# A recurrent condition and a routed FFN on one core: inputs on two queues, projections two blocks ahead, tanh straight into the next round's start, shared weights in halves

## What is computed

```python
def step(prev_h, xp_t):                  # recurrence; the state is 256 wide
    next_h = jnp.tanh(xp_t + prev_h @ Wh)
    return (next_h, next_h)
xp = einsum('ntd,dh->nth', x, Wx) + b    # x is (2, 1024, 256)
h = scan(step, h0, xp)                   # over the 1024 positions
# FFN on h: one shared expert and 8 routed ones, the best 2 of them for a token
shared = silu(h @ shared_w1.T) @ shared_w2.T
gates = softmax(top2(h @ gate_w.T))
selected = sum over the 2 experts e: gate_e * (silu(h @ w1_e) @ w2_e)
out = x + shared + selected
```

## Time and profile before

| | |
|---|---|
| timed runs | 383.47, 385.0, 388.58 us (median 385.0) |
| the profiled execution | 381.38 us, of it 379.7 us span |
| PE busy | 356.2 us, 94% |
| ACT busy | 244.1 us, 64% |
| DVE busy | 200.2 us, 53% |
| POOL busy | 108.5 us, 29% |

### The profile page before, as it was taken

The page is one execution under the profiler, slowest core; times in us unless marked ns, Lnnn a source line. Parts: engine busy times, 40 slices in busy tenths (PEclk is TensorE's granted clock), DMA queues, the critical chain, the costliest instruction groups (busy, mean ns, idle before and its releaser), DMA issues.

```text
span 379.7 us, 8904 instructions
## 1 busy us (share of the span) xinstructions
PE 356.2 (94%) x2458; PEld 253.0 (67%) x2459; DVE 200.2 (53%) x415; ACT 244.1 (64%) x478; POOL 108.5 (29%) x99
## 2 busy tenths in 40 slices
PE   5989999997997998999999999999999999999981
PEld 4758889964664675666667666667766666666660
DVE  0089999979996988964333323333323333232310
ACT  3777788888556778865555665556665556665530
POOL 1100010000276788600123333223333133332241
PEclk9999999999999999999999999999999999999996
DMA  6999999607697979999898998889988989989992
GB/s 194 422 421 434 428 407 334 194 4 124 87 199 182 225 180 226 235 194 196 176 129 153 168 155 155 147 149 156 158 149 154 148 142 158 148 159 147 152 127 28
DMA packets 158173, 73.50 MB, mean 194 GB/s; under 512 B 140736, under 2 KB 155200, under 8 KB 156992
## 3 DMA queue, kind: packets, MB, share of 16 engines
q1 hardware_dynamic: 146672, 59.83, 66.9%
q0 software_dynamic: 6864, 9.11, 16.9%
q10 hardware_dynamic: 4608, 4.20, 4.1%
HBM read 23.68 MB, written 16.53 MB: 106 GB/s over the span
## 4 chain that ended last, share of the span: by engine, by line
PE 80%; ACT 6%; DMA 5%; issue 3%; DVE 2%; another core or an unknown queue 1%; ACTq 1%; POOL 0%; SPq 0%; DVEq 0%; POOLq 0%
PE py L1138 32%; PE z L1033 30%; PE z L1047 8%; PE z L982 3%; PE z L1014 3%; DMA space<-recurrence_w 2%; DMA space<-space 2%; ACT space L799 1%; ACT space L876 1%; PE px L1025 1%; PE py L982 1%; PE z L995 1%; DMA space<-x_cols 1%; ACTq L896 1%
## 5 line engine op out<-in xcount | busy, mean ns | idle before, releaser
L1138 PE MATMUL py<-w_slots,space 128*128 (+1 forms) x1272 | 148.4, 273 | 7.4 <-DMA space<-recurrence_w 3.7
L1033 PE MATMUL z<-w_slots,x 128*128 (+1 forms) x636 | 145.9, 379 | 0.8 <-issue 0.8
L1138 PEld LDWEIGHTS py<-w_slots,space 128*128 128x128 f16 x1272 | 123.8, 98 | 33.1 <-issue 3.5
L1033 PEld LDWEIGHTS z<-w_slots,x 128*128 128x128 f16 x636 | 62.1, 98 | 65.0 <-issue 1.2
L453 POOL DMA_INDIRECT out<-space x37 | 57.5, 1553 | 157.0 <-issue 65.2
L876 ACT ACTIVATE space<-z,tile_scales 128x512 f32<-128x512 f32 x106 | 71.8, 678 | 41.3 <-PE z L1033 34.1
L582 DVE SCALAR_TENSOR_TENSOR recurrence_w<-space,tile_scales,recurrence_w 128x512 f16<-128x512 f32 x54 | 40.5, 750 | 71.7 <-ACT recurrence_w L881 65.6
L582 DVE SCALAR_TENSOR_TENSOR space<-space,tile_scales 128x512 f16<-128x512 f32 x52 | 39.0, 750 | 57.7 <-ACT space L881 42.4
L528 DVE SCALAR_TENSOR_TENSOR w_slots<-w_slots,w_scale 128x1024 f16<-128x1024 f32 x36 | 46.2, 1283 | 1.3 <-issue 0.3
L881 ACT ACTIVATE recurrence_w<-space,tile_scales 128x512 f16<-128x512 f32 x54 | 39.0, 722 | 8.7 <-ACT space L876 2.5
L430 POOL DMA_INDIRECT sorted_rows<-space x32 | 39.1, 1221 | 17.5 <-issue 13.1
(11 more groups left out here) (114 smaller groups left out, 178.9 us busy)
## 6 DMA issues: line engine op xcount, KB each, us to landing
w_slots<-weights SPq DMA_DIRECT2D x9, 2048.0 KB, 30.5
sorted_rows<-pad_row SPq DMA_DIRECT2D x1, 5070.0 KB, 60.2
space<-x_rows ACTq DMA_DIRECT2D x16, 128.0 KB
out<-space ACTq DMA_DIRECT2D x16, 128.0 KB
space<-x_cols SPq DMA_DIRECT2D x1, 1024.0 KB, 8.6
space<-recurrence_w SPq DMA_TRANSPOSE x54
space<-space SPq DMA_TRANSPOSE x52
x<-sorted_rows SPq DMA_TRANSPOSE x39
```

Source lines behind the costliest of these rows:

```text
L1033: last = nc.tensor.matmul(Z[u % 2][h][:], x16[:, u, x_part, k], weight(f, k * HID + h * BANK, BANK, part), start=k == 0 and x_part == 0 an ...
L1138: last = nc.tensor.matmul(PY[p][:, 0:D], hiddenT[:, p, low, q], weight(f, MATRIX + q * D, D, part), start=q == 0 and not low and part == 0 ...
```

## The change

- **Inputs.** ACT's queue now starts Wx, h0 and the bias; SP starts the first block of x at once. The last four blocks of x come in two transfers, and FFN 0's weights in two halves, each half between two transfers of x. The gate's weights come behind x and FFN 0.
- **Warm-up.** PE does six matmuls on a tile of ones before its first projection. POOL sets that tile first.
- **Round 0.** Four projections ahead of the first guess step; then PE does the guess step first and the projection of two blocks ahead behind it, and ACT does the two tanh first and `project_out` behind them.
- **Starts.** The last tanh of rounds 0 and 1 writes 126 columns straight to the next round's starting column. `next_start` on ACT and `start_ok` are gone, and PE waits for the tanh of each half.
- **Finding.** DVE finds FFN 0 in two halves and 6 of the 8 chunks of FFN 1. FFN 0 is reduced, scaled and its first split done alone, before FFN 1 is looked at. There are 7 batches in place of 6. ACT's finds begin 2 chunks earlier in the weights, so 10 chunks are left after round 2 in place of 8: one find of two chunks before tile 0, and one in each of tiles 1 to 4 (before: two, then tiles 1 and 2). ACT's loop in round 1 is written out. The scratch of the finds moves to the end of `space`.
- **Late scales and splits.** The last `find_scales` moves from g = 4 to g = 5 and stands with `route_scales`. Split 24 moves from g = 6 to g = 5 and is all DVE's; the ones behind it move up by one.

```diff
-ARRIVALS = ((0, 1), (1, 2), (2, 4), (4, BLOCKS))
+ARRIVALS = ((0, 1), (1, 2), (2, 4), (4, 6), (6, BLOCKS))
...
-EARLY_WIDES = 6 * WIDES - 2
-BOUND_BATCHES = ((0, 2), (2, 3), (3, 4), (4, 5), (5, 6), (6, FFNS))
-FOUND_BY_DVE = BOUND_BATCHES[0][1]
-WIDE_FINDS_FROM = FOUND_BY_DVE + L // CHUNKS
-SPLIT_FROM = 6
-LATE_WIDES = BOUND_BATCHES[-1][0] * WIDES
-LATE_SPLITS = tuple(range(LATE_WIDES + (3 * n + 1) // 2, LATE_WIDES + (3 * n + 4) // 2) for n in range(TILES - 2 - SPLIT_FROM))
+EARLY_WIDES = 22
+
+
+BOUND_BATCHES = ((0, 1), (1, 2), (2, 3), (3, 4), (4, 5), (5, 6), (6, FFNS))
+FOUND_BY_DVE = 2 * CHUNKS - 2
+WIDE_FINDS_FROM = FOUND_BY_DVE + L
+LATE_FINDS_FROM = WIDE_FINDS_FROM + 2 * L
+LATE_FINDS = (FFNS * CHUNKS - LATE_FINDS_FROM) // 2
+SPLITS_AT = {3: (22, 23), 5: (24,), 6: (25, 26), 7: (27,), 8: (28, 29), 9: (30,), 10: (31,), 11: (32, 33), 12: (34,), 13: (35,)}
+HIGHS_FROM = 6
...
-    return (min(f, WIDE_FINDS_FROM) - FOUND_BY_DVE) * CHUNKS + max(f - WIDE_FINDS_FROM, 0) * WIDES
+    return min(f * CHUNKS, WIDE_FINDS_FROM) - FOUND_BY_DVE + max(f * CHUNKS - WIDE_FINDS_FROM, 0) // 2
...
-        magnitudes = ys[:, 2:4].rearrange("p u d -> p (u d)").bitcast(BF16)
...
+        assert at[0] <= SPACE - CHUNK - 1
+        magnitudes = space[:, SPACE - CHUNK - 1:SPACE - 1].bitcast(BF16)
...
-            sp.dma_start(wx_sb, wx).then_inc(wx_in, 16)
...
+            load_x(0)
+            sp.dma_start(wh_sb, wh).then_inc(wh_in, 16)
+            load_x(1)
+            load_x(2)
+            load_weights(0, 0, CHUNKS // 2, w_up_in)
+            load_x(3)
+            load_weights(0, CHUNKS // 2, CHUNKS, w_in[0])
+            load_x(4)
             sp.dma_start(gate_sb[:], gate_cols).then_inc(gate_in, 16)
-            for f in range(FFNS):
-                sp.dma_start(w_slots[:, f * CHUNKS + 2:(f + 1) * CHUNKS + 2].rearrange("p s c -> p (s c)"),
-                             weights[f]).then_inc(w_in[f], 16)
+            for f in range(1, FFNS):
+                load_weights(f, 0, CHUNKS, w_in[f])
...
+            nc.gpsimd.memset(ones[:], 1.0).then_inc(consts, 1)
...
-                if n == 0:
-                    pool.wait_ge(bound_ok, 2)
-                else:
+                if n < 2:
+                    pool.wait_ge(bound_ok, n + 2)
+                if n > 0:
                     pool.wait_ge(found, found_upto(end))
...
-            for f in range(FOUND_BY_DVE):
-                last = find_largest(f)
-            last.then_inc(bound_ok, 1)
+            find_largest(0, 0, CHUNKS // 2, w_up_in)
+            find_largest(0, CHUNKS // 2, CHUNKS, w_in[0]).then_inc(bound_ok, 1)
             find_scales(0)
             link(nc.vector.tensor_copy(tile_scales[:, 0:TILES].rearrange("p t s -> p s t"),
                                        ffn_scales[:, :, 0:1].broadcast_to([P, 3, TILES])))
-            split_upto(FOUND_BY_DVE * WIDES)
+            split_upto(1)
+            find_largest(1, 0, FOUND_BY_DVE - CHUNKS, w_in[1]).then_inc(bound_ok, 1)
+            split_upto(WIDES)
...
-                elif g < TILES - 2:
-                    if g == 3:
-                        split_upto(LATE_WIDES)
-                    elif g == 4:
-                        find_scales(5)
-                        route_tiles()
-                    elif g == 5:
-                        route_scales()
+                elif g == 4:
+                    route_tiles()
+                elif g == LATE_FINDS:
+                    find_scales(len(BOUND_BATCHES) - 1)
+                    route_scales()
                 if g >= AHEAD:
                     shared_y(g - AHEAD)
-                if SPLIT_FROM <= g < TILES - 2:
-                    for c in LATE_SPLITS[g - SPLIT_FROM]:
-                        split(c, high_by_act=c in highs_by_act)
+                for c in SPLITS_AT.get(g, ()):
+                    split(c, high_by_act=c in highs_by_act)
...
+            nc.scalar.dma_start(wx_sb, wx).then_inc(wx_in, 16)
+            nc.scalar.dma_start(states[:, :, 0, 0:B], h0_cols).then_inc(h0_in, 16)
+            nc.scalar.dma_start(bias_sb[:], bias).then_inc(bias_in, 16)
...
-            for m in range(K):
-                project_out(0, m)
+            for n in range(K + 1):
+                project_out(n // K, n % K)
             for i in range(BLOCKS):
                 for u in range(2):
-                    if i + 1 < BLOCKS:
-                        project_out(i + 1, u)
                     for m in range(K):
                         act.wait_ge(z_mm[m], i * 2 + (u + 1))
-                        nc.scalar.activation(guess[:, 1 - u, m], ahead[i % 3][m][:, u * COLS:(u + 1) * COLS], ACT.Tanh,
-                                             bias=bias_sb[:, m:m + 1]).then_inc(h_ok[m], 1)
+                        if i * 2 + u + 1 == L:
+                            nc.scalar.activation(next_start(m), ahead[i % 3][m][:, u * COLS:(u + 1) * COLS - B], ACT.Tanh,
+                                                 bias=bias_sb[:, m:m + 1]).then_inc(h_ok[m], 1)
+                        else:
+                            nc.scalar.activation(guess[:, 1 - u, m], ahead[i % 3][m][:, u * COLS:(u + 1) * COLS], ACT.Tanh,
+                                                 bias=bias_sb[:, m:m + 1]).then_inc(h_ok[m], 1)
+                    n = i * K + u + K + 1
+                    if n < BLOCKS * K:
+                        project_out(n // K, n % K)
...
+                if c % CHUNKS == 0 or c == FOUND_BY_DVE:
+                    act.wait_ge(w_in[c // CHUNKS], 16)
...
-            def next_start(r, ends):
-
-                for k in range(K):
-                    act.wait_ge(h_ok[k], r * L)
-                act.sem_inc(act_waited, 1)
-                nc.scalar.copy(states[:, :, 0, B:COLS], ends[:, :, 0:COLS - B]).then_inc(start_ok, 1)
...
+                        if starts_next and u == 1:
+                            nc.scalar.activation(next_start(m), Z[p][m][:, u * COLS:(u + 1) * COLS - B], ACT.Tanh).then_inc(h[m], 1)
+                        else:
+                            nc.scalar.activation(column(m, i * 2 + u + 1), Z[p][m][:, u * COLS:(u + 1) * COLS], ACT.Tanh).then_inc(h[m], 1)
...
-                with act.Fori(0, steps // 2) as j:
-                    for p in range(2):
-                        step_pair(z_mm, h_ok, r, j * 2 + p, p, find_at, chunks)
-                for i in range(steps, L // 2 - 1):
-                    if i % steps == 0:
-                        act.wait_ge(w_in[first_found + i // steps], 16)
+                for i in range(L // 2 - 1):
...
-            act.wait_ge(w_in[LAST], 16)
-            for c in range(WIDES // 2):
-                act.wait_ge(found, found_upto(LAST) + c)
-                find_last(c)
+            find_last(0)
...
-                if g <= WIDES // 2:
-                    c = WIDES // 2 + g - 1
-                    act.wait_ge(found, found_upto(LAST) + c)
-                    find_last(c)
-                if SPLIT_FROM <= g < TILES - 2:
-                    c = highs_by_act[g - SPLIT_FROM]
+                if g < LATE_FINDS:
+                    find_last(g)
+                if g >= HIGHS_FROM and g in SPLITS_AT:
+                    if g == HIGHS_FROM:
+                        act.wait_ge(tiles_ok, 1)
+                    c = SPLITS_AT[g][0]
...
+            pe.wait_ge(consts, 1)
+            for _ in range(WARM_UP):
+                nc.tensor.matmul(PX1[:, 0:P], ones[:], ones[:], start=True, stop=True)
...
-            for m in range(K):
-                project(0, m)
+            for n in range(2 * K):
+                project(n // K, n % K)
             pe.wait_ge(guess_ok, 3)
             for i in range(BLOCKS):
                 for u in range(2):
-                    if i + 1 < BLOCKS:
-                        project(i + 1, u)
                     guess_step(i, u)
+                    if i + 2 < BLOCKS:
+                        project(i + 2, u)
...
+                        if k == 0 and (chained or u):
...
-                pe.wait_ge(start_ok, r)
...
-            pe.wait_ge(start_ok, SPECULATIVE_ROUNDS - 1)
```

46 lines of the change are left out of this document (21 added, 25 removed).

## The result

The changed kernel takes 389.5 us (median of 20 runs, 385.8 to 392.6), the kernel before in the same comparison 384.2 (20 runs). The ratio is 1.0136, 95% interval 1.0111 to 1.0160: 5.2 us slower, under 2% but clear of 1. The forecast was 383.9. The profiled execution took 388.2, its span 386.5 us (before 379.7).

The account below looks back on a forecast made before the run. PE and DVE together bound the time to the shared FFN, then the hand-over to the routed tiles: 3.0 us gained at the start, 1.9 returned, so 1.1 off, 383.9 against 385.0; range for 8 in 10, 378 to 388.

Parts of the forecast that it names:

- the hand-over: From POOL's last scatters to SP's loads of sorted rows and the routed tiles: returns 1.9 us of the gain.
- First projection at 3.8: Inputs: x's first block is issued one transfer earlier, so PE's first projection begins near 3.8 instead of 4.25.
- first guess step at 8.0: Warm-up: four projections cost 4.2 us, so the first guess step comes at 8.0 instead of 8.75, gain 0.75.
- slow bound: Warm-up without effect: the four projections ahead of the first guess step cost 6.0 us.
- 1.14 a step: Round 0: all 15 step intervals become short, 17.1 us in place of 18.46, gain 1.4.
- Starts and loop: Dropped copy lets round 1 begin 0.4 us earlier; ACT's written-out loop saves 0.11 at 8 positions, 0.9 us.
- end of the early splits at 76.6: DVE's early work takes 61 us from 15.5, ending at 76.6 instead of 79.68, gain 3.0, which decides.
- small waits: DVE's early work meets three waits, for FFN 1 and twice for ACT's finds, some 2 us.
- Finds and splits among the tiles at nothing: Shared FFN: moved finds and splits cost 0, covered by ACT's idle 4.98 us; up to 1.2 us otherwise.
- POOL: times right, consequence wrong: Last reduction near 108, first scatter 109.2, 5.8 us later than before; scatters end at 161.7 in place of 159.8.
- Gain up to here 3.0: Start of the shared FFN: tile 0's SiLU moves from 83.72 to 80.7, 3.0 us earlier.
- The slower one: Rival: POOL's late scatters make the hand-over cost more than the start gains, down(14) 2 to 3 us late, 387.5; 15%.

Follow-up runs that it names:

- a_one_queue: Changed kernel with Wx, x's first block, bias, Wh and h0 issued from SP in the old order; 1.0016 on chip 2, 1.0167 repeated on chip 3.
- after_again: Changed kernel unaltered, run again on chip 3; ratio 1.0126 to the kernel before.
- a_loop: Changed kernel with ACT's hardware loop over the first eight positions restored in both speculative rounds; ratio 1.0135 to the kernel before, chip 1.
- a_finds_early: Changed kernel with three finds ahead of tile 0 and one each behind tiles 1 and 2; ratio 1.0032 to the kernel before, chip 1.
- b_scatter_late: Kernel before with one added wait holding POOL's scatters until the fifth row tile is sorted out; ratio 1.0173, chip 2.
- a_spaced: Changed kernel with six chained POOL memsets behind each of the first 16 scatters; ratio 1.0493 to the kernel before, chip 2.
- after: The changed kernel itself as shown and profiled, against the kernel before; 389.5 us, ratio 1.0136.
- after_third: Changed kernel unaltered, run again on chip 4; ratio 1.0173 to the kernel before.
- a_reduce_between: Changed kernel with POOL's last reduction moved behind its first four scatters; ratio 1.0003 to the kernel before on chip 4, 0.9969 repeated on chip 5.

## Why the prediction was wrong

The step that failed is the one from the start of the shared FFN to the hand-over: the prediction let nothing in the tiles between hang on when the scatters run, and the runs showed 4 to 6.5 us there. The start was short too: of its gain of 3.0 us 0.84 came.

**First projection at 3.8: wrong.** It came at 5.04, and at 4.7 to 5.0 in the seven other profiles with two queues; in `a_one_queue` at 4.35. The forecast took one issue off and left the transfer's length as it was; from issue to use it grew from 3.0 to 4.2 us, with Wx on the other queue beside it and Wh and the second x behind it at once. That is what the Trainium skill (DMA: Bandwidth & Descriptors, "Issuing engines are not separate DMA queues") says of a second issuing engine; the trace agrees: one queue in the old order is back at 4.35. It goes further, since here the transfer that PE waits for lost 0.8 us.

**Warm-up, first guess step at 8.0: wrong here, right at times.** 10.46 in the profiled run, 5.42 us behind the first projection. In three of eight profiles with two queues the same four projections took 3.5 us (4.87 to 8.40 in `after_again`). The forecast's slow bound was 6.0, its value 4.2; the term measured 3.5 or 5.1 to 5.9, by the run.

**Round 0, 1.14 a step: right** (17.13 / 15). **Starts and loop: right.** Round 1 begins at 28.75, 1.16 behind the last guess step; from there PE reaches the end of round 2 some 1.2 earlier, for 0.9 forecast. But round 1 begins no earlier than before, since a first guess step 1.7 us late ate what round 0 and the start had won.

**DVE, end of the early splits at 76.6: wrong by 2.2, and this decided the start.** The half landed as said (15.41 against 15.5). Missing was POOL's first reduction, for which the sum has no term: before, it ran as soon as DVE was done, but there DVE was done only at 27.4. In the changed kernel POOL stood idle from 15 to 22.61 and DVE waited 5.34 us. The error is smaller than that because the 2 us of small waits that the sum did hold did not come. The gain at the first up was 0.84 in place of 3.0; in the other runs of the changed kernel PE waited there 1.4 to 1.5 us for DVE.

**Finds and splits among the tiles at nothing: right as priced,** PE had no wait from 90.85 to 119.2.

**POOL: times right, consequence wrong.** Reduction 109.5 for 108, first scatter 110.6 for 109.2, end 161.4 for 161.7. The forecast let this term cost only what the hand-over makes of it, 1.9 us. The hand-over cost nothing, and the late scatters 4 us (chip 1, `a_loop` 1.0135 against `a_finds_early` 1.0032) to 6.5 us (chip 4) in the tiles between. The step that failed is "Gain up to here 3.0", carried over from tile 0 to the hand-over as if nothing in the shared FFN hung on when the scatters run. The row to see it was there: ACT's 4.98 us with the releaser "remote" lay among the first eight scatters, and the text used it twice as cover for other work, and once as time that could only be won. A wait without a known cause is no cover, for what it hangs on may be what the change moves.

**The rivals.** The slower one had the right sign and engine and half the size (387.5, 2.5 us above 385.0, for 5.2), but its mechanism, a scatter that lands late, shows only in `b_scatter_late` and `a_spaced`, which issue their last at 166.19 and 178.73. The lock between DVE and POOL that it names fits the rows but is small: in `after` 15 scatters with a split or low part of DVE beside them take 1.33 us on average, the other 17 1.02, and the last still ends at 161.4. The range ended at 388; the measured ratio on its base of 385.0 is 390.2.

## What to carry to other kernels

When a change moves a step of POOL with its DMAs, price it against everything that runs beside it, and not only against its last consumer; and test that with one wait added to the kernel before, on more than one chip: on chip 2 a start at 111.9 cost nothing. An idle stretch whose releaser is "issue" or "remote" belongs in the sum as a cost that may grow. Ahead of a POOL instruction of a new kind, look whether its start-up time has been hidden so far: here an earlier consumer found it 5 us late.

## What the runs showed of the hardware

- **The stall.** On four chips of five (and in the runs shown), ACT's and PE's instructions come late among the scatters without a semaphore to wait for; on chip 2 they never did in four kernels. In the seven kernels off chip 2 whose finds and scatters are both late it begins 6.0 to 6.3 us behind the first scatter (`after`, `after_again`, `after_third`: 5.98, 5.97, 5.97) and lasts 6.6 to 12.1 us in one piece. This distance proves no link: it begins each time ahead of the same `sort_row`, the seventh, and does so in `a_reduce_between`, too, whose scatters start 7 us earlier. Meanwhile PE's instructions come 0.72 or 1.4 us apart, and the DMA engines are not full (share 0.62 in the window from 113.4). What it is remains open. Late fetching of the programs would look like it; the Trainium skill (Runtime: NRT & Kernel Launch, "Instruction fetch mechanics") says that each engine's sequencer fetches its next block by a DMA queue of its own, mostly hidden. No run here tells it apart: the profile's instruction packets fall at 101, 122.5, 124 and 133 us in `after`, and at 102.5, 121, 123 and 128 in `a_one_queue` on chip 2, which has no stall. And the changed kernel itself was not run on a chip without the stall: the nearest, `a_one_queue`, is level there (1.0016).
- **POOL's changes of kind of instruction.** The first `affine_select` begins at 8.8 to 10.0 us where the inputs come on one queue, and at 13.2 to 13.9 where they come on two, and there the reduction starts 6.8 to 8.5 us behind the last constant, though DVE had its part ready 3 to 6 us before.
- **The clock.** In five of eight profiles with the warm-up and two queues PE still ran its first four projections in 5.1 to 5.9 us (idle 0.92 to 1.04 us ahead of them), in three in 3.5 us (idle 0.75 to 0.93): the warm-up works or doesn't, at nearly the same gap. With one queue the gap was shorter, 0.19 to 0.35 us, and none of five profiles came under 4.25 us (4.25 to 5.41, two of them with 0.8 and 1.1 us of waiting for x inside). The granted clock reads 1.00 in this stretch in either case; that it is the clock is read from the single matmuls, 584 ns at the median in `after`, 379 in `after_again`.
